# Unrolling the feed-forward blocks on TensorE and putting the variant for exact weights first

## The reference

```python
x = x + _layernorm(_L0_attn_ref(_layernorm(x), Wq, bq, Wk, bk, Wv, bv, Wp, bp))
x = x + _layernorm(_L0_ffn_ref(_layernorm(x), w1_w, w1_s, w2_w, w2_s, h1_w, h1_s, h2_w, h2_s, w3_w, w3_s))

# attention: 16 heads of 16, every weight matrix replaced by mean(|W|) * sign(W) per row
# feed-forward, D_IN = 256, D_HID = 1024, weights drawn from {-1, 0, 1}:
h = silu(_tlin(x, w1_w, w1_s)) * _tlin(x, w2_w, w2_s)      # _tlin(x, w, s) = (x @ w.T) * s
h = gelu(_tlin(h, h1_w, h1_s), approximate=False)
h = gelu(_tlin(h, h2_w, h2_s), approximate=False)
return _tlin(h, w3_w, w3_s)
```

## Time and profile before

| quantity | value |
|---|---|
| median of 3 executions | 1320.01 us (1319.6 to 1320.9) |
| the profiled execution's own time | 1320.33 us |
| its span, first to last instruction | 1318.6 us |
| TensorE matmul busy | 1195.9 us (91%) |
| ScalarE (ACT) busy | 770.9 us (58%) |
| VectorE (DVE) busy | 558.4 us (42%) |
| mean granted TensorE clock | 0.967 |

### The profile page before, as it was taken

One profiled execution on the slowest core, in us unless ns is written; L12 is line 12 of the kernel. 1 busy time (PEld: TensorE's weight loads), 2 busy tenths in 40 slices (PEclk: granted clock), 3 DMA queues, 4 the chain that ended last, 5 costly groups with the idle time before them and its releaser, 6 DMA issues.

```text
span 1318.6 us, 19216 instructions
## 1 busy us (share of the span) xinstructions
PE 1195.9 (91%) x6696; PEld 734.9 (56%) x6696; DVE 558.4 (42%) x1013; ACT 770.9 (58%) x920; POOL 35.0 (3%) x30
## 2 busy tenths in 40 slices
PE   4965999999999999964999999989999999999997
PEld 3741222222222222212788888878888878888886
DVE  7941112111111112043664766727657457475633
ACT  4955999999999999964423324224342243332421
POOL 5220000000000000000000000000000000000000
PEclk9986999999999999977999999989999989999999
DMA  5998576667777776712000101001001001010000
GB/s 159 351 274 209 111 150 129 117 117 141 129 129 129 134 153 120 156 46 64 1 33 0 45 20 34 33 2 33 32 1 64 1 30 36 1 32 1 13 4 16
DMA packets 49946, 107.19 MB, mean 81 GB/s; under 512 B 5856, under 2 KB 22624, under 8 KB 49880
## 3 DMA queue, kind: packets, MB, share of 16 engines
q1 hardware_dynamic: 49880, 106.31, 34.8%
HBM read 71.91 MB, written 45.88 MB: 89 GB/s over the span
## 4 chain that ended last, share of the span: by engine, by line
PE 51%; DVE 1%; issue 1%; ACT 0%; DVEq 0%; ACTq 0%
PE ffn_ps L1136 23%; PE ffn_ps L1137 23%; PE ffn_ps L1164 2%; PE ffn_ps L1165 2%; PE side_ps L1120 1%; PE side_ps L1129 1%; DVE ln_stats L1273 0%; DVE zn L1284 0%; DVE zn L1325 0%; DVE x L1308 0%; DVE zn L1298 0%; DVE x_lo L1315 0%; DVE zn L1301 0%; DVE zn L1335 0%; DVE ln_mean_var L1277 0%
## 5 line engine op out<-in xcount | busy, mean ns | idle before, releaser
L912 ACT ACTIVATE probs<-s_ps 128x1024 f32<-128x1024 f32 x512 | 471.5, 1131 | 25.8 <-PE s_ps L863 25.7
L1137 PE MATMUL ffn_ps<-h_lo,W 128*128 128x512 f32 x1024 | 401.1, 392 | 0.0
L1136 PE MATMUL ffn_ps<-h_hi,W 128*128 128x512 f32 x1024 | 401.1, 392 | 0.0
L872 PE MATMUL y_ps<-probs,v_st 128*17 128x512 f32 x2048 | 273.1, 605 | 37.2 <-DVE y_sb L949 10.0
L1227 ACT ACTIVATE hid<-ffn_ps,scales 128x512 f32<-128x512 f32 x128 | 81.0, 685 | 232.6 <-PE ffn_ps L1137 227.7
L1136 PEld LDWEIGHTS ffn_ps<-h_hi,W 128*128 128x128 f32 x1024 | 192.4, 188 | 42.0
L1137 PEld LDWEIGHTS ffn_ps<-h_lo,W 128*128 128x128 f32 x1024 | 192.4, 188 | 42.0
L863 PEld LDWEIGHTS s_ps<-q_st,k_st 50*128 50x128 f32 x1024 | 78.7, 187 | 240.1 <-ACT probs L912 228.0
L863 PE MATMUL s_ps<-q_st,k_st 50*128 50x512 f32 x1024 | 194.4, 453 | 14.9 <-DVE y_ps L934 9.4
L941 DVE TENSOR_SCALAR low_bits<-W 128x1408 int32 (+1 forms) x16 | 14.3, 894 | 289.5 <-DMA W<-w_scr 289.5
L1349 DVE CAST h_hi<-hid 128x512 fp32r<-128x512 f32 x128 | 53.4, 417 | 183.7 <-ACT hid L1227 183.1
(11 more groups left out here) (103 smaller groups left out, 943.2 us busy)
## 6 DMA issues: line engine op xcount, KB each, us to landing
q_st<-q_scr SPq DMA_DIRECT2D x96, 128.0 KB, 6.7
k_st<-k_scr SPq DMA_DIRECT2D x96, 128.0 KB, 7.0
w_scr<-ffn_w SPq DMA_DIRECT2D x16, 704.0 KB, 12.7
W<-w_scr SPq DMA_DIRECT2D x16, 704.0 KB, 11.6
q_scr<-part SPq DMA_DIRECT2D x16, 512.0 KB, 5.7
k_scr<-part SPq DMA_DIRECT2D x16, 512.0 KB, 6.7
y_scr<-y_sb SPq DMA_DIRECT2D x16, 512.0 KB, 3.3
v_scr<-v_aug SPq DMA_DIRECT2D x8, 544.0 KB, 5.4
```

The source lines that it names most:

```text
L872: i = pe.matmul(y_ps[32 * j:32 * j + VCOLS, tb * BLK:(tb + 1) * BLK], v_st[u][:, s, VCOLS * j:VCOLS * (j + 1)], probs[m % 2][j // 2][:, j ...
L912: act.activation(probs[m % 2][pp][:, :, :], s_ps[a % 3][:, :, :], ACT.Exp, scale=SCALE).then_inc(probs_ready, 1)
L1136: pe.matmul(bank_of(t)[:, :], w, hi[:, k, :].bitcast(form), start=(k == 0), stop=False)
L1137: mm = pe.matmul(bank_of(t)[:, :], w, lo[:, k, :].bitcast(form), start=False, stop=last)
```

## The change

TensorE no longer uses `blocks`. Its eight steps are written out as straight code by a Python loop, with `i` a constant, for each of the two variants. The other engines keep `blocks` with its run-time loop. The flag is inverted (`all_exact`, true when the maximum of the low bits is not above 0), and the F32R variant now stands first, under `If`, and the F32 variant behind it, under `Else`. The work of each step and its order are the same.

```diff
-        any_low = sb("any_low", [1, 1], I32)
+        all_exact = sb("all_exact", [1, 1], I32)
...
             pe.wait_ge(bits_done, 3)
-            inexact = pe.value_load(any_low[:, :], min_val=0, max_val=1)
-            with pe.If(inexact):
+            def each_block():
+                for i in range(BLOCKS):
+                    step(i, i % 2, i + 1 < BLOCKS, i > 0)
+
+            exact = pe.value_load(all_exact[:, :], min_val=0, max_val=1)
+            with pe.If(exact):
+                form = F32R
+                each_block()
+            with pe.Else():
                 form = F32
-                blocks(pe, step, lambda: None)
-            with pe.Else():
-                form = F32R
-                blocks(pe, step, lambda: None)
+                each_block()
...
-            dve.tensor_scalar(any_low[:, :], top_bits[:, :], 0.0, None, ALU.is_gt).then_inc(bits_done, 1)
+            dve.tensor_scalar(all_exact[:, :], top_bits[:, :], 0.0, None, ALU.is_le).then_inc(bits_done, 1)
```

## The result

The changed kernel took 1303.02 us (median of 4 runs, 1302.1 to 1304.3) against 1320.45 us for the kernel before, a ratio of 0.9869 with a 95% interval of 0.9853 to 0.9886. Two later comparisons, each in its own session, gave 1304.46 us (0.9884, 0.9861 to 0.9907) and 1305.43 us (0.9893, 0.9877 to 0.9910). The three gains are 17.3, 15.3 and 14.1 us (1 less the ratio, times the kernel before), 15.6 on average, where the sum had 15.2.

A forecast was written before the change was run, and what follows sets the result against it. TensorE was taken to bound the kernel, idle in the feed-forward half only at its loop's two jumps back. Removing them was to save 15.2 us, all else nothing: 1320.0 - 15.2 = 1304.8 us, range 1303.3 to 1307.7.

The forecast's parts named there:

- the sum: Whole kernel: 15.2 us less, all from TensorE's two jumps, with every other part at nothing.
- The two jumps go: TensorE's two jumps back in the feed-forward loop: blocks with a jump cost 7.91 and 7.31 us more, together 15.2 us gained.
- The slow stretch: Rival, 6 in 100: TensorE's pace sags as from 1136 to 1189 us; one or two more stretches cost 1.1 to 2.3 us.
- worst case: Of the sag rival: the slow pace covers all 672 us of TensorE's work, costs 14 us and leaves 1318.
- The range: Whole kernel: 1303.3 to 1307.7 us, from the runs' scatter less 15.2, a sag possibly absent, and DVE's 2 us.
- The taken ones stand until new instructions arrive: TensorE's loop branch: the taken compare-and-branches, 3464 and 3679 ns, wait for instructions to be brought in.
- it makes no difference: Rival, 2 in 100: the loop body's code stays on the chip, TensorE's gaps have another cause and remain, 1320.0 us.
- DVE is late next: DVE's jumps at the same seams: 3 us lost, covered by 2.1 us, costing nothing; rival, 5 in 100: 2 us, 1306.8.
- The order of the variants: Entry of the exact variant: branch falls from 3345 to 83 ns, but the wait for `x2_lo` is unchanged, gain nothing.
- The new jump at the end: TensorE jumps over the F32 code after its last matmul: 3.7 us or twice that, hidden by at least 4 us.
- Straight code fetched in time: Rival, 4 in 100: TensorE's straight code is not fetched in time; six exposed packets cost 17.2 us, all 28 give 1385 us.

The follow-up runs named there:

- unroll_only: Kernel before with TensorE's blocks unrolled but the F32 variant still first and the exact one under Else: 1305.64 us, ratio 0.9901.
- all_engines_unrolled: Changed kernel with the loop written out on ACT, DVE and SP as well: 1302.85 us, ratio 0.9881 to the kernel before.
- before: The kernel before, with TensorE's run-time loop, in its first profile: 1320.45 us.
- before_again: The kernel before, unchanged, profiled a second time: 1319.8 us, ratio 1.0002.
- order_only: Kernel before with its loop kept on TensorE, only the flag and the order of the variants changed (exact first): 1316.73 us, ratio 0.9984.
- slot 96: Kernel before with the head of TensorE's exact-variant loop at instruction 96 of a fetch block: 1305.62 us, ratio 0.9893.
- slot 232: Kernel before with the head of TensorE's exact-variant loop at instruction 232 of a fetch block: 1312.19 us, ratio 0.9949.
- the three-step loop: Kernel before with TensorE's exact-variant loop as two rounds of three steps, head at instruction 0 of a block: 1307.65 us, ratio 0.9905.
- six_rounds: Kernel before with TensorE's exact-variant loop as six rounds of one step, five jumps back instead of two: 1303.97 us, ratio 0.9879.
- dve_late_by_two: Changed kernel with two added reciprocals on DVE at the start of each step, 3.5 us in all: 1310.13 us, run once.
- slots 0 and 32: Kernel before with the head of TensorE's exact-variant loop at instruction 0 or 32 of a fetch block: 1304.65 us (0.9884) and 1304.69 us (0.9889).
- hinted_loop: Kernel before with a prefetch hint on the jump back of TensorE's exact-variant loop: 1304.94 us, ratio 0.9889.
- hint_at_slot_96: Kernel before with TensorE's exact-variant loop head at instruction 96 of a block and a prefetch hint: 1305.39 us, ratio 0.9889.
- after: The changed kernel in its first comparison with the kernel before: 1303.02 us, ratio 0.9869.

## Why the prediction was right, and where it was wrong

**"The two jumps go", 15.2 us.** The mechanism as far as it was named (TensorE's own jumps, on the path, nothing else on it) held: every part of it was gone in the new trace and `unroll_only` shows that it is the unrolling. Its size was taken from one profile, and there the term was mis-sized: the jumps alone are 15.22 us in the first profile and 12.72 in the second. With the slow blocks, which the prediction did not count as a gain, it is 16.35 and 14.98 us, against a mean gain of 15.6 in the times and 15.2 from step 0 to the end. So 15.2 came out nearly right in part by luck: dear jumps in the one profile made up for the slow stretches left out.

**The slow stretch.** The prediction called the 53.22 instead of 52.09 us a sag that comes by itself, and feared more of it in a TensorE that never pauses. It is rather the other way round: it was in no profile of the changed kernel (three), `unroll_only` or `all_engines_unrolled`, and it followed 9 of 10 stalled jumps in the profiles of `before`, `before_again`, `order_only`, slot 96, slot 232 and the three-step loop. It is not tied to stalls alone: `six_rounds` has one before its first jump, slot 232 has one in block 0, and `dve_late_by_two`, unrolled on TensorE, has one before its first wait. So most of it belongs on the gain side, about 1.1 us per stalled jump. In it, matmuls of 512 columns start 0.233 us apart instead of 0.229 at full granted clock. Where it starts and ends is regular: behind 8 of these jumps it starts 76 to 81 us later, with the output layer after the next `turn_x1`, and only in the three-step loop directly behind the stall; it always ends at a `project_y`. That it is caused by the stall is not shown, and what it is stays open. (The prediction's worst case is also a little low: 2.17% of 672 us are 14.6 us, which leaves 1319.4 us, not 1318.)

**The range.** This is the step that failed. The lower end, 1303.3 us, counted the scatter of the three runs shown and one absent slow stretch, but put the scatter of the 627 us before step 0 at nothing beyond these three runs. Step 0 started between 624.7 and 629.7 us in the 18 profiles, 624.7, 628.2 and 628.9 in those of one and the same changed kernel. Behind that point the changed kernel is steady (675.4 to 675.8 us). Its profiled run in the first comparison is its fastest, 1302.09 us; for the median of 1303.02 us an estimate is 1303.02 - 1.8 (time over span) - 675.6 = 625.6 us for the start of step 0, about 2 us before the 627.5 us of the kernel before. In the other two comparisons the medians, 1304.5 and 1305.4 us, are in the range; so which side of its lower end the first one fell on was chance.

**The cause behind the price.** "The taken ones stand until new instructions arrive" was right: at each of the ten jumps back that stalled, in six profiles, a packet of TensorE's instruction queue starts 0.9 to 1.0 us behind the branch and takes 0.9 to 2.1 us, and the branch ends 1.3 to 1.5 us after it; behind none of the 14 free jumps is there a packet within 20 us, but for one that starts together with the first branch of `six_rounds`. Wrong was the answer to the rival "it makes no difference". The packets of the second and third round show only that the body did not stay on the chip in this placement: rounds that touch 4 or 5 blocks (`six_rounds`) and 7 (slots 0 and 32) kept their head, a round of 10.2 blocks lost it, and rounds that touch 8, without a hint, lost it at 9 of 10 jumps. The kernel before had its head 4 instructions before the end of a block, by what the trace records between the branch and the second gap, so its 1741 instructions touched eight blocks. The runs put the border there; why it lies there, and why a round of the kernel before takes 9 packets, they do not show. A branch to a resident target stands 207 to 261 ns and one to a missing target 3.3 to 4.4 us.

**DVE is late next, at no cost.** Right: 2.8 us lost on DVE, product 3.67 us after the scaling (forecast 3.6 to 3.9), no wait of TensorE, cover 2.4 to 2.7 us instead of 2.1, and no gain from unrolling DVE too.

**The order of the variants, at no cost.** Right for the entry: 73 ns instead of 3345, step 0 still behind `x_lo`. In the looped kernel the order did shift the code, which the prediction did not think of; that this changes the price of the jumps is not shown, since the 1.1 us in the profiles is within their scatter and the interval of the ratio 0.9984 just excludes 1.

**The new jump at the end.** Right: it begins at 1288.5 us, stands 3.5 us and ends 4.9 us before the last store is issued.

**Straight code fetched in time.** Right: 37 packets on the page, no gap in any of the unrolled kernels.

## What to carry to other kernels

Before unrolling a run-time loop on an engine, look at its compare-and-branch and at the instruction packets of later rounds. Here the taken branch stood 3.3 to 3.7 us and 9 packets came in the second round: the head of the body was fetched again; shortening the body (one step instead of two) or placing its head so that it touches one block less gave the whole gain with a loop. A jump that stalls can cost more than its gaps (6.0 to 7.9 us for 3.9 to 4.8 us of them, where the granted clock fell to 0.50 behind them), and a size read from one profile carries the scatter of the parts that the change does not touch.

## What the runs showed of the hardware

- TensorE's jump back cost nothing when its target was resident: the branch stands 207 to 261 ns, no packet follows it, and the first matmul behind it starts 1.92 or 1.93 us after the branch (14 jumps in `hinted_loop`, `six_rounds`, `hint_at_slot_96` and slots 0, 32 and 96). When it was not, it cost 2.4 to 3.0 us where the granted clock stayed at 1.00 (idle for 1.8 to 2.4 us, slots 96 and 232) and 5.4 to 7.9 us with two gaps of together 3.2 to 4.8 us and a granted clock of 0.50 for 3.4 to 6.9 us (head 4 or 11 instructions before the end of a block, `before`, `before_again` and `order_only`). The three-step loop, with one gap of 2.6 us and a clock of 0.50 for 3.4 us, lies between (5.25 us).
- TensorE's code came in packets of 16.4 KB, 256 instructions each (slot 232 and the 24 instructions up to the second gap). A round of 1741 recorded instructions stayed resident with its head at instruction 0 or 32 of a block (no packet in the second and third round), lost it at one jump of two at 96 (branches of 4098 and 219 ns), and at both at 232 (3312 and 3633 ns).
- At a granted clock of 1.00 TensorE has a second pace, 0.233 us per 512 columns instead of 0.229, that lasts 46 to 53 us at a time here (about 1.1 us lost: a block of 84.4 instead of 83.3 us), mostly starting within 81 us behind a stall.
- ACT's table load takes 1.28 us (`after`, L1242); before the first gate of a step inside ACT's run-time loop it stood behind a wait of 7.22 us for the first tile, in straight code (`all_engines_unrolled`) it ran 7 us earlier.
